# A three-layer attention network on one core: transposing an activation through VectorE's 32x32 blocks and adding transfers instead of through TensorE

## What is computed

```python
def gat(inp, mask, W, a):                      # softmax over neighbours
    h = inp @ W
    e = leaky_relu((h @ a1)[:, :, None] + (h @ a2)[:, None, :], 0.2)
    e = where(mask > 0, e, -9e15)              # the first layer has no mask
    return elu(softmax(e, axis=2) @ h)

h   = maximum(layernorm(x), 0)
o1  = relu(h @ mlp1_w + mlp1_b)                # 128 -> 256
z   = elu(gat(o1, None, W_fc, a_fc)) + o1      # layer 1, width 256
o2  = relu(z @ mlp2_w + mlp2_b)                # 256 -> 128
y   = relu(elu(gat(o2, adj, W_hand, a_hand)) + o2)
x   = x + y
h   = maximum(layernorm(x), 0)
x   = x + gat(h, adj, W, a)                    # layer 3, width 128
```

## Time and profile before

| | |
|---|---|
| median of 3 runs | 432.97 us (431.36 to 433.53) |
| span of the profiled execution, first to last instruction | 429.0 us |
| median less span | 4.0 us |
| PE busy | 411.1 us, 96% |
| DVE busy | 357.8 us, 83% |
| ACT busy | 315.7 us, 74% |
| POOL busy | 24.9 us, 6% |
| DMA moved | 36.42 MB, mean 85 GB/s |

### The profile page before, as it was taken

The page is one execution under the profiler, slowest core; times in us unless marked ns, Lnnn a source line. Parts: engine busy times, 40 slices in busy tenths (PEclk is TensorE's granted clock), DMA queues, the critical chain, the costliest instruction groups (busy, mean ns, idle before and its releaser), DMA issues.

```text
span 429.0 us, 8704 instructions
## 1 busy us (share of the span) xinstructions
PE 411.1 (96%) x2544; PEld 352.7 (82%) x2544; DVE 357.8 (83%) x1226; ACT 315.7 (74%) x764; POOL 24.9 (6%) x53
## 2 busy tenths in 40 slices
PE   6999999999999999999999999999999999989782
PEld 4688779887898899797998788989879799869772
DVE  7786588878998898988898868979698899889974
ACT  2655659658796787786878688687867887799774
POOL 0000000000001000010100000100000000000000
PEclk9999999999999999999999999999999999999997
DMA  7854323123423142232222213222320122120001
GB/s 209 278 146 130 105 74 121 74 76 98 125 98 75 53 138 84 52 101 74 75 82 68 75 53 98 79 72 74 80 87 10 49 93 59 45 80 24 27 1 57
DMA packets 39461, 36.42 MB, mean 85 GB/s; under 512 B 4080, under 2 KB 30320, under 8 KB 39408
## 3 DMA queue, kind: packets, MB, share of 16 engines
q1 hardware_dynamic: 37408, 33.17, 26.1%
q10 hardware_dynamic: 2000, 2.63, 1.8%
HBM read 31.46 MB, written 4.32 MB: 83 GB/s over the span
## 4 chain that ended last, share of the span: by engine, by line
PE 87%; DVE 5%; ACT 3%; issue 2%; DMA 1%; SPq 0%; POOL 0%; ACTq 0%; DVEq 0%
PE bank L1530 24%; PE bank L1437 23%; PE bank L1426 13%; PE bank L1416 6%; PE bank L1477 6%; PE bank L1455 6%; PE bank L1445 3%; PE bank L1538 2%; PE bank L1496 1%; PE bank L1466 1%; DMA row<-row_scratch 1%; DVE stats L1036 1%; DVE u L1265 1%; ACT ext L826 1%; ACT e L911 1%
## 5 line engine op out<-in xcount | busy, mean ns | idle before, releaser
L1530 PEld LDWEIGHTS bank<-ext,prob 128*128 128x128 f32 x1024 | 119.6, 192 | 6.3 <-issue 4.9
L1530 PE MATMUL bank<-ext,prob 128*128 128x129 f32 x1024 | 122.1, 275 | 0.3 <-DVE prob L1207 0.2
L1437 PE MATMUL bank<-ext,prob 128*128 128x257 f32 x512 | 119.0, 380 | 0.0
L1437 PEld LDWEIGHTS bank<-ext,prob 128*128 128x128 f32 x512 | 94.8, 190 | 17.3 <-issue 4.5
L1211 DVE SCALAR_TENSOR_TENSOR prob<-prob,square,mask_t 128x512 f32<-128x512 f32 x98 | 70.6, 739 | 0.9 <-ACT prob L859 0.8
L1426 PE MATMUL bank<-wfc_sb,o_t 128*128 128x259 f32 x256 | 64.0, 382 | 0.4 <-ACT o_t L790 0.4
L859 ACT ACTIVATE prob<-row,square 128x512 f32<-128x512 f32 x78 | 54.1, 720 | 0.1
L1426 PEld LDWEIGHTS bank<-wfc_sb,o_t 128*128 128x128 f32 x256 | 46.3, 190 | 9.6 <-issue 4.5
L903 ACT ACTIVATE y<-bank,recip 128x128 f32<-128x128 f32 x128 | 39.3, 369 | 15.3 <-DVE recip L1257 14.2
L911 ACT ACTIVATE e<-y,minus_one 128x512 f32<-128x512 f32 (+1 forms) x70 | 47.7, 688 | 1.4
L1265 DVE SCALAR_TENSOR_TENSOR u<-e,y 128x512 f32<-128x512 f32 (+1 forms) x70 | 44.1, 638 | 4.2 <-issue 2.2
(11 more groups left out here) (98 smaller groups left out, 499.1 us busy)
## 6 DMA issues: line engine op xcount, KB each, us to landing
row<-row_scratch SPq DMA_DIRECT2D x36, 256.0 KB, 3.3
moments_row<-moments_scratch SPq DMA_DIRECT2D x13, 512.0 KB, 3.8
x_in<-in_x SPq DMA_DIRECT2D x16, 256.0 KB, 5.3
x_res<-in_x SPq DMA_DIRECT2D x16, 256.0 KB, 4.6
out<-y_out SPq DMA_DIRECT2D x15, 256.0 KB, 3.9
normed<-in_x_t SPq DMA_DIRECT2D x14, 256.0 KB, 4.3
row_scratch<-square_t SPq DMA_DIRECT2D x144, 0.5 KB
adj_sb<-in_adj ACTq DMA_DIRECT2D x1, 1024.0 KB, 8.1
```

The source lines that it names most:

```text
L1437: last = nc.tensor.matmul(filled[:, 0:H + 1], gat1.targets(b, t, c), gat1.features_and_one(b, t), start=(t == 0), stop=(t == C - 1))
L1530: last = nc.tensor.matmul(filled[:, e * (D + 3):e * (D + 3) + D + 1], L.targets(b, t, c), L.features_and_one(b, t), start=(t == 0), stop=( ...
```

## The change

For batches 2 to 12 (`MOVED`) PE no longer turns `u`. In place of `z_0`, `z_1` of such a batch:

- VectorE transposes each half of `u` within 32x32 blocks (`turnu_0`, `turnu_1`) into `u_turned`.
- GpSimd writes `u_turned` to DRAM in four transfers of 32 partitions each (`move`), which puts the blocks in their places, waits until all four have landed, and loads 512 KB back with a transfer that adds to `o1_t` (`move_in`). These wait in GpSimd's list, between the maxima.
- `o1_t` then holds o1 plus `u`, and `mlp2` reads it after the adding transfer has landed. In these batches `o1_t` is stored in an order of nodes by blocks of 32, and ScalarE's `mlp1`, the row of layer 1 and the moving operand of `mlp2` have access patterns to match.

In batches 0, 1, 13, 14 and 15 PE still turns `u`, and VectorE adds in place in `o1_t` (no `z_t`). The minus one of elu moves for all batches into the bias of `mlp2`, by column sums of `w2` that PE makes once (`sums_w2`). `o1_t` has four buffers in place of three. The second loads of x and the results are issued by GpSimd and no longer by SP. The five lists of `ORDER` are new throughout.

```diff
-O1_DEPTH = 3
+O1_DEPTH = 4
+MOVED = tuple(range(2, 13))
...
+            def write_blocks(b):
+                pool.wait_ge(*u_blocks.at(b, 2))
+                if b.n - 2 in MOVED:
+                    pool.wait_ge(*z_moved.two_back(b))
+                places = blocks_scratch[b.slot].rearrange("(f j a n) -> a j f n", f=HT * ROWS, j=32, a=ROWS)
+                for a in range(ROWS):
+                    pool.dma_start(places[a], u_turned[32 * a:32 * (a + 1)].rearrange("p f c i -> p f (c i)")).then_inc(
+                        blocks_written.sem(b), 16)
+
+            def add_blocks(b):
+                pool.wait_ge(*blocks_written.landed(b))
+                pool.wait_ge(*s1.h_filled.at(b, C))
+                pool.dma_start(o1_t[:, b.of(O1_DEPTH)], blocks_scratch[b.slot].rearrange("(k p n) -> p k n", k=HT, p=P),
+                               accum_op=ALU.add).then_inc(z_moved.sem(b), 16)
...
+            def turn_blocks(b, part):
+                r = slice(part * C // 2, (part + 1) * C // 2)
+                dve.wait_ge(*s1.u.at(b, part + 1))
+                earlier = [n for n in MOVED if n < b.n]
+                if part == 0 and earlier:
+                    dve.wait_ge(*blocks_written.landed(Batch.nth(earlier[-1])))
+                nc.vector.transpose(u_turned[:, :, r].rearrange("p f c i -> p c f i"),
+                                    gat1.u[:, r].rearrange("p c (f i) -> p c f i", i=32)).then_inc(u_blocks.sem, 1)
...
             def residual1(b, f):
                 dve.wait_ge(*z_filled.at(b, f + 1))
-                if b.first > 0 and f == 0:
-                    dve.wait_ge(*o2_filled.two_back(b))
-                nc.vector.scalar_tensor_tensor(out=z_t[:, b.slot, f], in0=bank_of(f"z_{f}", b)[:], scalar=-1.0,
-                                               in1=o1_t[:, b.of(O1_DEPTH), f], op0=ALU.add, op1=ALU.add).then_inc(
-                    z_ready.sem, 1)
+                o1 = o1_t[:, b.of(O1_DEPTH), f]
+                nc.vector.tensor_tensor(o1, bank_of(f"z_{f}", b)[:], o1, ALU.add).then_inc(z_ready.sem, 1)
...
             def mlp2(b):
                 if b.first == 0:
                     pe.wait_ge(s_w2, 16)
-                pe.wait_ge(*z_ready.at(b, HT))
+                pe.wait_ge(*(z_moved.landed(b) if moved(b) else z_ready.at(b, HT)))
                 filled = free("mlp2", b)
                 for k in range(HT):
-                    last = nc.tensor.matmul(filled[:], w2_sb[:, k], z_t[:, b.slot, k],
+                    z = o1_t[:, b.of(O1_DEPTH), k]
+                    last = nc.tensor.matmul(filled[:], w2_sb[:, k], by_blocks(z) if moved(b) else z,
                                             start=(k == 0), stop=(k == HT - 1))
                 last.then_inc(o2_filled.sem, 1)
```

More of the change, by code:

```diff
@@ L48 @@
     "sync": """
[L49 to L53, removed]
@@ L60 @@
+        load_t.15 row1.12 row3.8 row1.13 row3.9 row0.15 row2.11 row3.10 row2.12 row1.14 row3.11 row1.15 row3.12
     """,
     "gpsimd": """
[L62 to L65, removed]
+        load_again.1 max1.0 max1.1 max1.2 max1.3 max2.0 max2.1 max1.4 move.2 load_again.0 move_in.2 move.3 max1.5
@@ new lines @@
+        prob1_1.2 prob1_2.2 prob1_3.2 max2.0 norm1.7 args1.3 z_0.1 att1_0.2 z_1.1 row1.3 att1_1.2 args2.0 att1_2.2
+        stats1.9 prob2_0.0 prob2_1.0 max2.1 att1_3.2 args2.1 prob2_2.0 prob2_3.0 prob2_0.1 prob1_0.3 prob1_1.3
+        elu1_0.2 turnu_0.2 prob1_2.3 prob1_3.3 max1.4 att2_0.0 att2_1.0 elu1_1.2 args1.4 turnu_1.2 normt.6 prob2_1.1
+        prob2_2.1 prob2_3.1 att1_0.3 att1_1.3 row1.4 norm1.8 norm1.9 elu2.0 att1_2.3 x1.0 att1_3.3 norm2.0 root2n.0
+        att2_0.1 prob1_0.4 elu1_0.3 turnu_0.3 att2_1.1 stats1.10 elu1_1.3 prob1_1.4 prob1_2.4 prob1_3.4 turnu_1.3
@@ new lines @@
+        sums_w2 mlp2.0 h1_0.3 h1_1.3 h1_2.3 row1.2 h2_0.0 h1_3.3 h2_1.0 mlp1_0.4 mlp1_1.4 z_0.1 z_1.1 att1_0.2
+        att1_1.2 mlp2.1 att1_2.2 row2.0 h2_0.1 h2_1.1 att1_3.2 h1_0.4 h1_1.4 h1_2.4 row2.1 h1_3.4 att2_0.0 att2_1.0
+        mlp1_0.5 mlp1_1.5 att1_0.3 att1_1.3 att1_2.3 turn_o2.0 att1_3.3 att2_0.1 att2_1.1 mlp2.2 turn2.0 h1_0.5
+        h2_0.2 h2_1.2 h1_1.5 h1_2.5 h3_0.0 turn_o2.1 h1_3.5 h3_1.0 att1_0.4 att1_1.4 att1_2.4 turn2.1 att1_3.4
+        h3_0.1 h3_1.1 mlp2.3 mlp1_0.6 mlp1_1.6 row3.0 h2_0.3 h2_1.3 att1_0.5 att1_1.5 att1_2.5 att1_3.5 att3_0.0
@@ new lines @@
+        z_1.13 turn_o2.11 h1_0.14 h1_1.14 h1_2.14 h1_3.14 h1_0.15 mlp2.13 turn2.11 h1_1.15 h1_2.15 h1_3.15 h3_0.11
+        h2_0.13 h2_1.13 h3_1.11 att3_0.10 att3_1.10 row2.13 att2_0.12 att2_1.12 att1_0.14 turn_o2.12 att1_1.14
+        att1_2.14 att1_3.14 att2_0.13 turn2.12 att2_1.13 h3_0.12 h3_1.12 att3_0.11 att3_1.11 z_0.14 z_1.14 att1_0.15
+        att1_1.15 turn_o2.13 att1_2.15 att1_3.15 mlp2.14 turn2.13 h2_0.14 h2_1.14 h3_0.13 h3_1.13 z_0.15 z_1.15
+        att3_0.12 row2.14 mlp2.15 row3.13 att3_1.12 h2_0.15 h2_1.15 att2_0.14 att2_1.14 turn_o2.14 row2.15 att3_0.13
@@ L555, in gnn_program @@
             "scores23": lambda b: (s_wa, 9),
+            "sums_w2": lambda b: (s_wa, 10),
         }
@@ L1378, in score_columns23, with sums_w2 @@
                                             start=True, stop=True)
+                last.then_inc(s_waf, 1)
+            def sums_w2(b):
+                pe.wait_ge(s_w2, 16)
+                filled = free("sums_w2", b)
+                for k in range(HT):
+                    last = nc.tensor.matmul(filled[:, 0:1], w2_sb[:, k], score_scale[:, 1, 0:1],
+                                            start=(k == 0), stop=(k == HT - 1))
                 last.then_inc(s_waf, 1)
```

406 lines of the change are left out of this document (213 added, 193 removed).

## The result

The changed kernel takes 456.65 us in the median of 4 runs (454.86 to 459.95), the kernel before 432.79 us beside it. The ratio is 1.0572, with an interval of 1.0523 to 1.0622: 5.7% slower, far outside the range of 422 to 437 us.

What follows compares the result with a forecast made beforehand. PE's work was taken to bound the kernel from 20 to 370 us. Span 429.0 - 9.4 + 2.7 + 1.1 = 423.4 us, plus 4.0 for the runs' median, gave 427.4 us, 1.3% faster; range 422 to 437.

Steps and rivals of the forecast that it cites:

- Both I price at nothing: Issues shifted from SP to GpSimd, and 11 x 1 MB more DMA traffic at mean share 0.28: both at zero cost.
- the row on the chain in the drain: One row through DRAM on the drain's chain for 4.43 us, the only place where SP's relief could tell.
- The path, 11.5 us: From turnu_1's end through GpSimd's issues, write landing and adding load's landing, before mlp2: 11.5 us, bounds 8.7 to 23.
- The room: PE's other work covering the path before mlp2: about 10.3 to 11 us for five batches, 12 to 15 for six.
- The loss at `mlp2`, 2.7 us: PE's wait at mlp2 where path exceeds room: 1.2 us plus 3 x 0.5, 2.7 us in all.
- Rival 1: Path longer than room, PE waits at mlp2: 12.2 us lost at a 13.5 us path, median 436.9; chance 16%.
- PE full, so that 9.4 us of work removed are 9.4 us gained: PE sets the time; dropping eleven batches' transposes of u, less sums_w2, shortens the span by 9.4 us.
- The maxima, 1.1 us: GpSimd's maxima wait behind moves, delaying VectorE's args and the softmax: 0.1 us a batch on PE, 1.1 us.
- rival 3: GpSimd's whole list late, VectorE stopping at args: 11 us in place of 1.1, ending at 437; chance 8%.
- Rival 2: VectorE's 533 ns instructions block GpSimd's descriptor writing, some 4 us lost, 431, no measurable change; chance 12%.
- The block transpose, 709 ns: Each 128x512 block transpose of u on VectorE takes 709 ns by a slope; 22 of them 15.6 us.
- A stall long enough to lower the clock: A PE stall lowering the granted clock, 1.00 up to 370 us, would cost far more than its own length.

Runs made afterwards that it cites:

- e1_no_wait: Changed kernel with adding loads sent to a tile nobody reads and mlp2 of batches 2 to 12 waiting only for the block transposes; 449.42 us, ratio 1.0382.
- e2_no_moves: e1_no_wait without issuing the block writes and adding loads or waiting for them; new order and late transfers on GpSimd stay; 428.26 us, ratio 0.9915.
- e4_old_order_in_place: Kernel before, same lists and no moved batch, with only addition in place, a fourth o1_t buffer and the mlp2 bias; 432.58 us, ratio 1.0021.
- e11_three_moved: Whole computation in the order of the kernel before, late transfers on SP, only batches 2, 3 and 8 moved; 438.67 us, ratio 1.0173.
- e8_an_eighth: e1_no_wait with all its transfers and waits but an eighth of the bytes in each write and adding load; 428.34 us, ratio 0.9899.
- e9_rows_late: e2_no_moves with four extra 0.5 KB writes by SP ahead of the writes of every row of batches 2 to 12; 451.57 us, ratio 1.0441.
- e7_plain_loads: e1_no_wait with the eleven 512 KB adding loads made plain loads; 438.43 us, ratio 1.0132.
- e10_small_packets: e1_no_wait with each adding load cut into 512 B pieces in place of 2 KB, same bytes; 452.97 us, ratio 1.0456.

## Why the prediction was wrong

Taken from the ratios of the runs, the way from the kernel before to the changed one is +0.9 us (addition in place), -4.6 (new order without the moves), +20.2 (the moves' traffic) and +8.2 (PE's wait for the adding loads): 24.7 us in all. The prediction had nothing, -9.4, nothing and +2.7 for these, and +1.1 for the maxima.

- **"Both I price at nothing": the DMA traffic, with contention that "adds tenths to landings".** This is the step that failed, and it cost 20.2 us. The eleven moves bring 11.5 MB over the same 16 DMA engines. I looked at the mean share of 0.28 and asked whether the bandwidth would do. The rows need little bandwidth, but they need to pass promptly, 36 times, each through two transfers in turn, and their writes landed later: SP waited for them 67.6 us in e1_no_wait and 46.0 in e2_no_moves. The only sign that I weighed was the row on the chain in the drain, and I took it for a matter of the drain alone.
- **The path, 11.5 us.** It was 13.1 in the mean of the eleven (11.4 to 15.6). Four issues took 2.4 us where I had 3.5; the writes landed after the last issue by 2.2 to 4.6; two hand-overs of 0.3 each weren't in the sum; the adding load took 5.9 to 7.6 us from its issue on where I had 0.9 + 4.4. In batch 10 the adding load waited 4.5 us behind a maximum in GpSimd's list, which itself waited for VectorE. The room, up to the start of the last product ahead of `mlp2`, was within 1 us of what I had for batches 3, 5, 7 and 9, but shorter for 2, 8 and 11: 9.5, 10.8 and 10.5 us where I had 12 to 15.
- **The loss at `mlp2`, 2.7 us.** 15.3 us of excess stand there in the trace, but taking the wait away gave back 8.2 (uncertainty 3.2). At least a part of the rest came back at another place: ahead of `h2` PE waits for ScalarE's copy of `mlp2` (L970, in e1_no_wait L975), 3.6 us in the changed kernel and 8.1 without the wait, and ScalarE is the engine that waits most for rows:

```profile
PE bank L1556 <- ACT o_t L970: 3.6, 4, 1.7
...
PE bank L1564 <- ACT o_t L975: 8.1, 6, 2.1
```

  Rival 1 was the nearest in mechanism (12.2 us at a path of 13.5), but it ended at 436.9, since it too left the traffic out.
- **PE full, so that 9.4 us of work removed are 9.4 us gained.** From e4_old_order_in_place to e2_no_moves I measure 4.6 us. PE did lose the work, but the new order itself has small gaps, 8.5 us of excess against 5.6 for the old one even without the moves, and rows at 6.02 us against 5.84. It had also used up the slack of the rows before any move was added: ScalarE and VectorE wait for rows 15.7 us in e2_no_moves and 0.5 in e4_old_order_in_place, and still only 2.7 in e11_three_moved, where "row" is 6.03 us. The traffic of the moves met an order that had little slack for it. With the transfers free the plan would have gained a percent.
- **The maxima, 1.1 us; rival 3.** The rival is refuted, and the term was small as forecast: VectorE waits 2.3 us in all for maxima, against 1.3 before, and e8_an_eighth has the whole list of GpSimd at no cost that can be measured.
- **Rival 2, VectorE's 533 ns instructions hold up GpSimd's issues.** Refuted for this kernel: 44 issues of writes take 582 to 762 ns. One held for as long as such an instruction would stand some 500 above the lowest, and none does, though 13 of them ran while one of these instructions did, with a mean of 616 ns against 603 for the others. The rule of the Trainium skill (SBUF — State Buffer) isn't refuted by that, since nothing here shows which mode these instructions ran in.
- **The block transpose, 709 ns:** 700. That step, and the slope that it came from, held.
- **A stall long enough to lower the clock.** This happened, three times between 20 and 400 us, but it didn't cost "far more than its own length". The windows are behind PE's waits of 3.9 us at 91, of 2.2 us at 240 and of 3.1 us at 265 (columns as above):

```profile
91.00:95.00 4.00, 3.90 (x8) 1.99 (x9) 2.85 (x11) 0.54 (x1) 0.00 (x0) 0.57 0.29 105
...
240.00:250.00 10.00, 9.63 (x46) 7.26 (x47) 5.88 (x22) 5.64 (x15) 0.00 (x0) 0.83 0.00 1
...
266.00:270.00 4.00, 4.00 (x10) 1.59 (x8) 1.34 (x3) 0.76 (x2) 2.33 (x4) 0.61 0.84 227
```

The granted clock was 1.00 from 230 to 240 and 0.99 from 255 to 266 us, and 0.61 in the mean of the four microseconds from 266 on, that is partly at 1.2 GHz. The four records of `mlp2` there follow one another after 0.85 to 0.91 us, where 0.43 is usual for 512 columns, so this place cost some 1.7 us beyond the wait, and three of them some 5 us, an estimate. Between 20 and 400 us the profile of e1_no_wait has two such places, that of e9_rows_late two and that of e2_no_moves none, so by this estimate some 3.4 of the 20.2 us between e1_no_wait and e2_no_moves are clock. Over the whole run the mean clock is 0.983 against 0.994 before.

## What to carry to other kernels

Before moving work to DMA, list the small transfers on which the critical engine depends, with how many hops each makes and how much room each has, and price what one large transfer beside each of them costs; the mean DMA share and the medians of landings don't show it. A wait in a trace names who stood last, not what its removal would give: keep all the traffic and take only the wait away, then keep the waits and take only the bytes away, and the two runs separate the causes. Count what a new order does to the slack of other paths before anything is added to it. And work taken off a full engine pays only as far as the new order keeps it full.

## What the runs showed of the hardware

- A transfer that adds is dear beyond its bytes: the same 512 KB took 6.3 us to land in place of 4.1 and 1.23 us of GpSimd's issue in place of 0.72, and it cost the rest of the kernel 10.8 us more over eleven of them (e1_no_wait less e7_plain_loads). The Trainium skill (DMA: Bandwidth & Descriptors, on the anatomy of one DMA) fits a GpSimd transfer by 2.0 us plus its bytes at 436 GB/s, an estimate of 3.2 us for 512 KB; the plain one took 0.9 us more here and the adding one twice that estimate.
- Transfers issued by GpSimd in its queue delay those of SP's queue although these are other queues: SP's wait for the 0.5 KB writes of 36 rows rose from 46.0 us (e2_no_moves) to 67.6 (e1_no_wait), and in the place shown above from 0.98 us for one row to 5.36 for the next, beside an adding load. The effect goes with the bytes and the adding, not with the number of transfers or of their packets: an eighth of the bytes in as many transfers cost nothing that can be measured (e8_an_eighth), and four times the packets for the same bytes made no measurable difference (e10_small_packets).
- GpSimd issues a 32-partition write in 0.60 us and a 512 KB adding load in 1.23, less and more than the 0.87 that I took from its maxima.
- A wait of PE of 2.2 to 3.9 us in an otherwise full stretch was followed by a granted clock of 0.57, 0.60 and 0.61 in the mean of the 4 us from 91, 242 and 266 us, and by 512-column records 0.85 us apart in place of 0.43.
